# Y-direction hats spread by DMA, weights on VectorE, copies on ScalarE, and 64x64 attention products

## The chip, the cores and the metric

The kernel runs on one core of one Trainium2 chip. The metric is the time of one execution on the device in microseconds (us); lower is better. Engines are named as in the profile: PE is TensorE's matmul, PEld its weight load, DVE is VectorE, ACT is ScalarE, POOL is GpSimd, SP issues the DMAs.

## The reference

The input x is (8, 64, 32, 32): 8 images, 64 channels. Two deformable 3x3 convolutions, then attention and an expert layer on the 1024 pixels of each image as tokens:

```python
off1 = conv2d(x, w_off1, b_off1, stride=1, pad=1)
out = relu(bn_inf(deform_conv(x, off1, w_dc1, 1, 2, 2), g1, beta1, m1, v1))
off2 = conv2d(out, w_off2, b_off2, stride=1, pad=1)
out = relu(bn_inf(deform_conv(out, off2, w_dc2, 1, 2, 2), g2, beta2, m2, v2) + x)
t = to_tokens(out)
t = t + attention(layer_norm(t))      # 8 heads, each token sees the 32 tokens up to its own
t = t + experts(layer_norm(t))        # 32 experts, 8 tokens each per image
```

`deform_conv` reads, for each pixel and each of 9 taps (spaced 2 apart), the image at a place moved by that pixel's own offsets (dy, dx), by bilinear interpolation, and multiplies the 9 samples of 64 channels with a 576x64 matrix.

## The kernel before

**Sampling as a product.** The bilinear weight of a source pixel is a hat in x times a hat in y: with a distance d, min(|d|, 1) - 1 in either direction, so that the signs cancel. The image is cut into tiles of 4 rows by 8 columns (32 pixels, `TR` = 8 tile rows, `TC` = 4 tile columns). A *unit* is one ky of the taps and 4 output rows at most; there are 25 in a convolution, in threes (ky = 1, 0, 2), and three make one row of 4 output rows. A unit has two *strips* in the main (one per tile row that its offsets reach; offsets under 1 pixel are taken for granted, and a flag set by the largest offset leads to a general path `all_*` that does not run here). For each strip:

- `columns_pe` (L186): PE makes x distances into a pair of PSUM banks of a ring of two pairs; ACT takes their absolute value into `hx` (L384), DVE makes the hats (L428).
- `rows_pe` (L204): the same for y distances, with ACT at L390 and DVE at L431. These are made again in every unit, for 128 partitions (32 source pixels by 4 images), though all 8 columns of a source row share them.
- `weigh` (L357): hats in x times hats in y, DVE for one half of the images (g = 0) and POOL for the other (g = 1).
- `sample` (L301): 32 matmuls, source pixels by 64 channels against the weights, into PSUM banks 0 to 3. In the trace an f32 matmul is two records, so a strip is 64.
- `take` (L334): ACT copies banks 0 and 1 to SBUF, DVE banks 2 and 3. The banks are there once, so PE starts the next unit after both.

After the middle unit of a row, from unit 4 on, comes the *final* of the row before (`final_pe`, L234: 36 matmuls, 72 records; the second convolution adds the residual, L241), and ACT applies the normalization (L1418, L1424). In the first convolution PE also turns each finished row into source tiles (L262).

**Order.** Everything is an order written out by hand per engine. `Plan` makes the list of ring items ("x", "y", "f" for final, "t" for turn); PE starts `unit.inside` between the products of a unit and `unit.behind` after them. An item waits for the one two places before it to be emptied (two ring slots). While a unit is sampled, the hats of the second next are made. Ahead of the sampler, `offsets_*` convolve the offsets, split them in three bf16 parts, and move these through DRAM into the layout of `off`.

**Attention.** 32 blocks in a loop of four per turn. A block's PE work is `queries` (L856: 8 products of 64x128 weights), a mask (L869), `scores` (L879: 16 products, 64x128 weights, 64 columns), `values` (L923) for two images, `turn_probs` (L904), `turn_keys` (L892), `project_values` (L938). Blocks overlap: PE turns probabilities one block ahead, scores are further ahead. DVE subtracts the maximum (L1042, L1044) and sums; ACT does the exponential (L991) and copies values (L1003) out of PSUM.

Of the kernel before, what the change touches and what calls it, by code (L numbers as in the profile page):

```python
# [71 lines left out]
class Strip:  # L72


    def __init__(self, tile_row, first, n):
        self.tile_row, self.first, self.n = tile_row, first, n


class Unit:
    def __init__(self, u, strips_before):  # L80
# [4 lines left out]
        for tile_row in range(TR):  # L85
# [3 lines left out]
            if last > first:  # L89
                self.strips.append(Strip(tile_row, first - self.base, last - first))  # L90
# [4 lines left out]
        self.y_items = []  # L95
        for strip in sorted(self.strips, key=lambda strip: -strip.n):
            for item in self.y_items:
                if sum(a.n for a in item) + strip.n <= UNIT_ROWS:
                    item.append(strip)
                    break  # L100
            else:
                self.y_items.append([strip])
        at = 0
        for item in self.y_items:
            for strip in item:
                strip.at = at
                at += strip.n
        self.hat_rows = at
        self.coords = [("x", u, 0), ("x", u, 1)] + [("y", u, k) for k in range(len(self.y_items))]


class Plan:
# [6 lines left out]
    def __init__(self, turns):  # L119
# [6 lines left out]
        for unit in self.units:  # L126
            todo = self.units[unit.u + 2].coords if unit.u + 2 < len(UNITS) else []
            final = [("f", unit.u // 3 - 1)] if unit.u % 3 == 1 and unit.u >= 4 else []
            turn = [("t", unit.u // 3 - 2)] if turns and unit.u % 3 == 1 and unit.u >= 7 else []
            cut = len(todo) if final else (len(todo) + 1) // 2  # L130
            unit.inside, unit.behind = todo[:cut], todo[cut:] + final + turn
            if unit.u == len(UNITS) - 1:
                unit.behind = unit.behind + [("f", TR - 1)]
                if turns:
                    unit.behind = unit.behind + [("t", TR - 2), ("t", TR - 1)]
# [57 lines left out]
def rows_pe(nc, m, cv, bank, u, strips):  # L193

    base, ky = UNITS[u]
    for strip in strips:
        for first, n in offset_parts(base + strip.first, strip.n):
            for g in range(2):
                rows = group_rows(g, 0)
# [1644 lines left out]
```

## Time and profile before

| | us |
|---|---|
| median of 3 runs (725.22 to 732.11) | 725.85 |
| the profiled execution, its span | 730.97, 729.2 |
| loads and first offset convolution | 0 to 37.9 |
| first sampler | 37.9 to 203 |
| second offset convolution | 203 to 232.6 |
| second sampler | 232.6 to 391 |
| layer norm, folded head weights | 391 to 419 |
| attention (its loop from 448) | 419 to 662 |
| experts | 662 to 729 |

The stages are read from the first and last instructions of their lines. PE is busy 80% of the span, DVE 64%, ACT 50%, POOL 40%. The mean granted TensorE clock is 0.865 of the upper level (2.4 GHz); the lower level is half of it, so a mean of 0.75 says that half of the time was spent there.

### The profile page before, as it was taken

How to read it: one execution, taken by the hardware profiler on the slowest of the kernel's cores; microseconds unless marked ns; L12 is line 12 of the kernel's file. 1: busy time of each engine (PE TensorE's matmuls, PEld its weight loads, DVE VectorE, ACT ScalarE, POOL GpSimd, SP SyncE). 2: the span in 40 equal slices, each digit the busy share in tenths (PEclk: the TensorE clock that was granted, in tenths of full speed). 3: DMA queues.
4: the chain of work that ended last, by engine and by line, in shares of the span. 5: the costliest groups of instructions: out<-in, count | busy, mean ns of one | idle time of the engine just before them, and what ended most of it. 6: DMA issues, size and time to landing. Idle time of an engine off the chain costs nothing.

```text
span 729.2 us, 28608 instructions
## 1 busy us (share of the span) xinstructions
PE 584.0 (80%) x12986; PEld 436.3 (60%) x12986; DVE 464.4 (64%) x554; ACT 361.7 (50%) x558; POOL 291.9 (40%) x275
## 2 busy tenths in 40 slices
PE   5668878887875787778776597999999999994556
PEld 1156666665532666556655486888888888873343
DVE  0578877886306889788854525666666766666544
ACT  0265656665214656455552434655656656554522
POOL 4046656665100556665640504344344343330400
PEclk9958979988787589899999556999999999998769
DMA  8320000000004000000001800000000000000002
GB/s 307 75 38 3 4 4 4 4 4 3 4 4 90 12 4 4 3 4 4 4 4 35 234 1 2 3 0 0 0 0 0 0 0 0 0 1 1 1 1 117
DMA packets 6395, 17.85 MB, mean 24 GB/s; under 512 B 1869, under 2 KB 4237, under 8 KB 5573
## 3 DMA queue, kind: packets, MB, share of 16 engines
q1 hardware_dynamic: 6286, 16.24, 8.0%
q8 instruction: 87, 1.43, 0.8%
q14 instruction: 22, 0.18, 0.1%
HBM read 12.37 MB, written 3.87 MB: 22 GB/s over the span
## 4 chain that ended last, share of the span: by engine, by line
PE 63%; DVE 17%; ACT 8%; issue 6%; DMA 3%; POOL 1%; SPq 1%; DVEq 0%; POOLq 0%; ACTq 0%
PE banks L301 13%; PE banks L879 9%; PE banks L234 9%; PE banks L856 5%; PE banks L923 5%; PE banks L904 5%; DVE y L357 5%; PE banks L938 4%; ACT hy L390 3%; DVE y L334 3%; PE banks L650 2%; DMA off<-in_places_dram 2%; DVE hy L431 2%; PE banks L869 2%; ACT hx L384 1%
## 5 line engine op out<-in xcount | busy, mean ns | idle before, releaser
L357 POOL TENSOR_TENSOR y<-hy,hx 128x576 f32<-128x576 f32 (+1 forms) x92 | 166.9, 1832 | 183.4 <-DVE hy L431 180.9
L301 PE MATMUL banks<-y,xt 32*64 32x144 f32 (+1 forms) x5888 | 148.2, 326 | 54.2 <-DVE y L334 42.5
L301 PEld LDWEIGHTS banks<-y,xt 32*64 32x64 f32 x5888 | 126.5, 151 | 71.4 <-issue 54.1
L357 DVE TENSOR_TENSOR y<-hy,hx 128x576 f32<-128x576 f32 (+1 forms) x92 | 113.2, 1268 | 5.1 <-PE banks L301 0.5
L1120 POOL TENSOR_TENSOR y<-y,stats 128x1024 f32<-128x1024 f32 x32 | 60.9, 1902 | 109.1 <-DVE stats L1052 109.0
L384 ACT ACTIVATE hx<-banks 128x576 f32<-128x576 f32 x100 | 65.0, 654 | 67.7 <-PE banks L186 64.6
L1042 DVE TENSOR_REDUCE stats<-banks 128x16 f32<-128x1024 f32 x32 | 39.2, 1225 | 69.5 <-PE banks L879 69.5
L234 PE MATMUL banks<-y,w_dc 64*64 64x256 f32 x1152 | 76.7, 424 | 3.7 <-DVE y L334 2.3
L390 ACT ACTIVATE hy<-banks 128x768 f32<-128x768 f32 (+1 forms) x92 | 70.4, 812 | 14.3 <-PE banks L204 13.9
L334 DVE COPY y<-banks 128x768 f32<-128x768 f32 x50 | 47.6, 952 | 46.6 <-PE banks L301 46.4
L879 PEld LDWEIGHTS banks<-src,y 64*128 64x128 f32 x1024 | 64.5, 201 | 7.9 <-issue 7.9
L879 PE MATMUL banks<-src,y 64*128 64x64 f32 x1024 | 69.1, 289 | 0.0
L1003 ACT COPY hy<-banks 128x512 f32<-128x512 f32 x64 | 38.0, 593 | 62.6 <-PE banks L923 62.6
L234 PEld LDWEIGHTS banks<-y,w_dc 64*64 64x64 f32 x1152 | 47.5, 152 | 30.9 <-issue 12.2
L431 DVE TENSOR_SCALAR hy<-hy 128x1632 f32<-128x1632 f32 (+2 forms) x50 | 45.9, 918 | 11.5 <-ACT hy L390 11.4
L204 PE MATMUL banks<-off,sel 14*64 14x384 bf16 (+1 forms) x384 | 43.5, 378 | 9.5 <-ACT hx L384 7.8
L428 DVE TENSOR_SCALAR hx<-hx 128x1152 f32<-128x1152 f32 x50 | 44.7, 894 | 6.3 <-ACT hx L384 6.3
L991 ACT ACTIVATE y<-y 128x1024 f32<-128x1024 f32 x32 | 33.9, 1059 | 27.1 <-DVE y L1044 27.1
L1050 DVE TENSOR_REDUCE stats<-y 128x16 f32<-128x1024 f32 x32 | 39.0, 1218 | 12.9 <-ACT y L991 12.9
L186 PE MATMUL banks<-off,sel 14*64 14x144 bf16 (+1 forms) x832 | 40.6, 254 | 6.4 <-issue 6.1
L904 PE MATMUL banks<-identity,y 128*128 128x128 f32 x256 | 42.9, 291 | 3.1 <-ACT hy L997 3.1
L923 PE MATMUL banks<-hy 64*64 64x128 f32 x1024 | 42.9, 282 | 1.7 <-ACT hy L1003 1.7
(141 smaller groups left out, 836.1 us busy)
## 6 DMA issues: line engine op xcount, KB each, us to landing
src<-in_x_dram SPq DMA_DIRECT2D x4, 578.0 KB, 5.7
y<-in_w_dram SPq DMA_DIRECT2D x1, 2080.0 KB
xt<-in_xt_dram SPq DMA_DIRECT2D x1, 2048.0 KB, 11.4
off<-in_w_dram SPq DMA_DIRECT2D x2, 1024.0 KB
out_dram<-tokens SPq DMA_DIRECT2D x4, 512.0 KB, 2.6
offsets_dram<-tokens SPq DMA_DIRECT2D x32, 54.0 KB
off<-offsets_dram SPq DMA_DIRECT2D x16, 108.0 KB
w_dc<-in_w_dc_dram SPq DMA_DIRECT2D x2, 288.0 KB, 8.8
```

The costliest lines, as they stand in the source:

```text
L234: last = nc.tensor.matmul(out, cv.w_dc[rows, tap, :], moving, start=(tap == 0), stop=(tap == TAPS - 1 and cv.k == 0), skip_group_check=True)
L301: last = nc.tensor.matmul(ap(out, [[UNIT_ROWS * PITCH - 2, 3], [PITCH, strip.n], [1, WIN_COLS]]), m.xt[32 * j:32 * j + 32, strip.tile_row, ...
L334: return copy(ap(m.sampled[:, unit.ky, unit.slot if unit.ky == 1 else unit.base // UNIT_ROWS % 2, j, 0, :], [[3 * PLACES, 2], [W, 3 * UNIT ...
L357: multiply(dst, hy, hx, ALU.mult).then_inc(cv.s_ready[g], 1)
L384: nc.scalar.activation(ap(m.hx[:, u % 2, 0, side * item[2]:], [[X_HATS, 2], [2 * side, 3], [1, side]]), ap(m.ps[:, bank, :], [[BANK, 2], [ ...
L390: nc.scalar.activation(ap(m.hy[:, u % 2, 0, strips[0].at * HAT_ROW:], [[Y_HATS, 2], [HAT_PITCH, 3 * n_rows], [1, W]]), ap(m.ps[:, bank, :] ...
L428: nc.vector.tensor_scalar(hat, hat, 1.0, 1.0, ALU.min, ALU.subtract).then_inc(cv.hats, 1)
L431: nc.vector.tensor_scalar(hat, hat, 1.0, 1.0, ALU.min, ALU.subtract).then_inc(cv.hats, 1)
L879: last = nc.tensor.matmul(m.ps[:, 2 + hg, first:first + KEYS], at.g[rows, b % 2, image, j, :], keys[rows, b % 4, j * TQ:j * TQ + KEYS], st ...
L904: last = nc.tensor.transpose(m.ps[:, 4, k * P:(k + 1) * P], at.p[:, b % SLOTS_P, hg, image, odd, :], m.identity[:, :])
L923: last = nc.tensor.matmul(m.ps[C * hg:C * hg + C, 5 + late, first:first + P], at.xw[rows, b % 2, odd, C * image:C * image + C], at.pt[rows ...
L1120: nc.gpsimd.tensor_tensor(p, p, scale.unsqueeze(2).to_broadcast([P, 2 * TILES * HG, KEYS]), ALU.mult).then_inc(at.probs_ready, 1)
```

## The change

**Hats in y once per source row.** `rows_pe` and its items are gone. The offsets in f32 go to DRAM as they are (`dump_offsets`), and 96 partitions (4 source rows of a tile, 8 images, 3 kx) read a chunk of 8 output rows; ACT takes |distance| with a bias from a new table `hy_bias` (8 instructions a chunk, 4 chunks), DVE makes the hats (one instruction), SP writes them to DRAM (`write_chunk`) and reads them per unit, each source row's into the partitions of its 8 columns (`read_unit`: two DMAs of 128 x 816 f32, 418 KB each), into three slots.

**Weights and copies.** DVE does all products of `weigh`; POOL none. ACT copies all four banks, but for every third unit, in which DVE copies two.

**Order.** PE samples a unit in one piece; the x items, the final and (one place later than the final) the turn stand behind it.

**Attention.** The products of `queries`, mask and `scores` are halved to 64x64 weights, and PE's waits for queries, scores and the second image's values are gathered before the last transposition of the first image's probabilities.

```diff
-            cut = len(todo) if final else (len(todo) + 1) // 2
-            unit.inside, unit.behind = todo[:cut], todo[cut:] + final + turn
+            row, phase = unit.u // 3 - 1, unit.u % 3
+            final = [("f", row)] if row >= 0 and phase == 1 else []
+            turn = [("t", row)] if turns and row >= 0 and phase == 2 else []
+            unit.inside, unit.behind = [], todo + final + turn
...
         elif item[0] == "f":
-            for taker in range(2):
-                pe.wait_ge(cv.taken[taker], 3 * (item[1] + 1) + 1)
+            pe.wait_ge(cv.taken, 2 * (3 * (item[1] + 1) + 1))
...
+def takers(unit):
+
+    return "av" if unit.u % 3 == 2 else "aa"
+
+
+def weigh(nc, dve, m, cv, unit):
+
+    dve.wait_ge(cv.hy_loaded[unit.u % HAT_SLOTS], 2 * 16 * (unit.u // HAT_SLOTS + 1))
+    dve.wait_ge(cv.hats, unit.u + 1)
+    for strip in unit.strips:
...
+        for g in range(2):
...
+            nc.vector.tensor_tensor(dst, hy, hx, ALU.mult).then_inc(cv.s_ready, 1)
...
-        take(nc.scalar.copy, m, cv, unit, 0).then_inc(cv.taken[0], 1)
+        take(nc.scalar.copy, m, cv, unit, 0).then_inc(cv.taken, 1)
+        if takers(unit) == "aa":
+            take(nc.scalar.copy, m, cv, unit, 2).then_inc(cv.taken, 1)
         for _ in unit.behind:
             item_act(n)
             n += 1
+        chunk, step = divmod(unit.u, UNITS_PER_CHUNK)
+        if chunk + 1 < CHUNKS_Y and step < 2:
+            chunk_distances(nc, act, m, cv, chunk + 1, step)
...
+    for row in range(TILE_ROWS):
+        col = 2 * row + lower
+        nc.scalar.activation(
+            ap(m.hat[0:COMPACT, row * ROW_HATS + lower * HAT_ROW:], [[TILE_ROWS * ROW_HATS, 2], [HAT_PITCH, 3], [1, W]]),
+            ap(m.hyin[0:COMPACT, row * W:], [[TILE_ROWS * W, 2], [CHUNK_ROWS * W, 3], [1, W]]),
+            ACT.Abs, bias=m.hy_bias[0:COMPACT, col:col + 1]).then_inc(cv.near, 1)
...
+        if bank == 1:
...
+            for lower in range(2):
+                chunk_distances(nc, act, m, cv, 0, lower)
...
+    def read_unit(u):
...
+            sp.wait_ge(cv.s_ready, 2 * cv.plan.units[u - HAT_SLOTS + 1].before)
...
+            source = bass.AP(at.tensor, at.offset, [[plane, 16], [0, TILE_COLS], [1, n * ROW_HATS]])
+            sp.dma_start(m.hy[:, u % HAT_SLOTS, g, first * ROW_HATS:(first + n) * ROW_HATS], source
+                         ).then_inc(cv.hy_loaded[u % HAT_SLOTS], 16)
...
-                    last = nc.tensor.matmul(m.ps[:, 2 + hg, first:first + KEYS], at.g[rows, b % 2, image, j, :],
-                                            keys[rows, b % 4, j * TQ:j * TQ + KEYS], start=False, stop=True,
-                                            skip_group_check=True)
+                    for side in range(2):
+                        half = slice(C * side, C * side + C)
+                        last = nc.tensor.matmul(m.ps[half, 2 + hg, first:first + KEYS], at.g[rows, b % 2, image, j, half],
+                                                keys[rows, b % 4, j * TQ:j * TQ + KEYS], start=False, stop=True,
+                                                skip_group_check=True)
...
+    def before_products(i, b):
+
+        if exists(i, b + QUERIES_AHEAD):
+            before_queries(i, b + QUERIES_AHEAD)
+        if exists(i, b + SCORES_AHEAD):
+            before_scores(i, b + SCORES_AHEAD)
+        before_values(i, b, 1)
```

Line numbers move: L301 becomes L271, L186 L183, L234 L208, L334 L298, L384 L353, L428 L407, L357 L328; in attention L856 becomes L914, L869 L933, L879 L943, L923 L989, L904 L970. New are L391 (ACT, chunk distances) and L400 (DVE, chunk hats).

DVE in the second sampler, one unit, before: `hx` and `hy` hats, two weights (the other two are POOL's), the copy.

```order
L428 TENSOR_SCALAR hx<-hx 128x1152 [waits c1_emptied]
L431 TENSOR_SCALAR hy<-hy 128x1632 [waits c1_emptied]
L357 TENSOR_TENSOR y<-hy,hx 128x576 [waits c1_hats,c1_sampled]
L357 TENSOR_TENSOR y<-hy,hx 128x576 [waits c1_sampled]
L334 COPY y<-banks 128x768 [waits c1_sampled]
```

And now, two units; the semaphores `c1_hy_loaded0` to `2` are the DMA's into the three slots:

```order
L407 TENSOR_SCALAR hx<-hx 128x1152 [waits c1_emptied]
L328 TENSOR_TENSOR y<-hy,hx 128x576 [waits c1_sampled,c1_hats,c1_hy_loaded2]
L328 TENSOR_TENSOR y<-hy,hx 128x576
L328 TENSOR_TENSOR y<-hy,hx 128x576 [waits c1_sampled]
L328 TENSOR_TENSOR y<-hy,hx 128x576
L407 TENSOR_SCALAR hx<-hx 128x1152 [waits c1_emptied]
L328 TENSOR_TENSOR y<-hy,hx 128x576 [waits c1_sampled,c1_hats,c1_hy_loaded0]
L328 TENSOR_TENSOR y<-hy,hx 128x576
L328 TENSOR_TENSOR y<-hy,hx 128x576 [waits c1_sampled]
L328 TENSOR_TENSOR y<-hy,hx 128x576
L298 COPY y<-banks 128x768 [waits c1_sampled]
```

The `hy` hats are gone from DVE, the products are four instead of two, and the copy stands in one unit of three.

PE around a final of the second sampler before (L234); `banks<-y,xt` are samplings, `banks<-off,sel` distances:

```order
L301 MATMUL banks<-y,xt 64x3x4x12 [waits c1_s_ready1,c1_s_ready0]
L301 MATMUL banks<-y,xt 64x3x4x12 x15
L204 MATMUL banks<-off,sel 64x3x2x32 [waits c1_emptied]
L204 MATMUL banks<-off,sel 64x3x2x32 x7
L301 MATMUL banks<-y,xt 64x3x4x12 x16
L204 MATMUL banks<-off,sel 64x3x2x32 [waits c1_emptied]
L204 MATMUL banks<-off,sel 64x3x2x32 x7
L234 MATMUL banks<-y,w_dc 64x2x128 [waits c1_taken1,c1_taken0,c1_emptied]
```

And the same place now:

```order
L271 MATMUL banks<-y,xt 64x3x4x12 [waits c1_s_ready]
L271 MATMUL banks<-y,xt 64x3x4x12 x31
L183 MATMUL banks<-off,sel 64x3x24 [waits c1_moved1,c1_emptied]
L183 MATMUL banks<-off,sel 64x3x24 x15
L183 MATMUL banks<-off,sel 64x3x24 [waits c1_emptied]
L183 MATMUL banks<-off,sel 64x3x24 x15
L208 MATMUL banks<-y,w_dc 64x2x128 [waits c1_taken,c1_emptied]
```

The distances no longer stand between samplings, and the ring slot that the final waits for (`c1_emptied`) is now the first x item's of the same unit, which ACT empties after its copies.

PE in the attention loop before, from the queries to the scores:

```order
L856 MATMUL banks<-src,s 128x128 [waits at_z_ready,at_xw_ready,at_pt_ready]
L923 MATMUL banks<-hy 64x128 x8
L900 REGISTER_ALU [waits at_probs_ready]
L904 MATMUL banks<-identity,y 128x128 [waits at_pt_ready]
L904 MATMUL banks<-identity,y 128x128 x3
L863 REGISTER_ALU
L869 MATMUL banks<-mask,spread_q 128x512 [waits at_shifted,at_swapped_ready,at_g_ready]
L869 MATMUL banks<-mask,spread_q 128x512
L879 MATMUL banks<-src,y 128x64 x15
L910 REGISTER_ALU
L879 MATMUL banks<-src,y 128x64 [waits at_z_ready,at_pt_ready]
L923 MATMUL banks<-hy 64x128 x8
```

And now:

```order
L970 MATMUL banks<-identity,y 128x128 [waits at_pt_ready]
L970 MATMUL banks<-identity,y 128x128 x2
L903 REGISTER_ALU
L905 ISA [waits at_windows_ready]
L922 ISA [waits at_g_ready]
L976 ISA [waits at_shifted,at_swapped_ready,at_g_ready]
L970 MATMUL banks<-identity,y 128x128 [waits at_z_ready,at_pt_ready]
L914 MATMUL banks<-src,s 64x128 x16
L933 MATMUL banks<-mask,spread_q 64x512 x4
L943 MATMUL banks<-src,y 64x64 x32
```

The wait for `z_ready`, ACT's copy of the first image's values, stood at the last score product; it now stands before queries, mask and all scores.

## Rows read from the trace of the kernel before

**Rows 1.** Windows: us, PE, PEld, DVE, ACT, POOL busy, PEclk, DMA share, GB/s

```profile
8.00:12.00 4.00, 1.11 (x16) 0.44 (x24) 0.00 (x0) 0.00 (x0) 0.71 (x1) 1.00 1.06 441
66.89:184.29 117.40, 95.27 (x3206) 71.94 (x3204) 91.87 (x89) 68.00 (x100) 71.58 (x60) 0.86 0.02 4
264.03:377.54 113.51, 88.63 (x3232) 67.25 (x3232) 91.79 (x89) 64.69 (x95) 65.92 (x36) 0.92 0.02 4
419.40:448.00 28.60, 23.91 (x180) 19.96 (x180) 12.10 (x14) 9.12 (x13) 5.09 (x9) 0.50 0.01 1
448.00:640.00 192.00, 192.00 (x2966) 156.99 (x2966) 124.07 (x163) 115.67 (x194) 78.20 (x110) 0.99 0.00 0
```

**Rows 2.** Timeline, one row of the second sampler: start, us, instruction [idle <-releaser]

```profile
288.27 0.96 DVE L334 COPY y<-banks 128x768 f32<-128x768 f32 x1 [0.36 <-PE banks L301]
...
289.01 1.54 ACT L390 ACTIVATE hy<-banks 128x768 f32<-128x768 f32 x2
...
290.58 1.01 DVE L431 TENSOR_SCALAR hy<-hy 128x1632 f32<-128x1632 f32 x1 [0.69 <-ACT hy L390]
...
291.70 2.56 DVE L357 TENSOR_TENSOR y<-hy,hx 128x576 f32<-128x576 f32 x2
...
295.22 0.78 PE L301 MATMUL banks<-y,xt 32*64 32x144 f32 x32 [2.70 <-DVE y L334]
```

**Rows 3.** Groups by shape, ACT: busy us, mean ns of one | idle before

```profile
L384 ACT ACTIVATE hx<-banks 128x576 f32<-128x576 f32 x100 | 65.0, 654 | 67.7 <-PE banks L186 64.6 <-PE banks L204 1.2
...
L334 ACT COPY y<-banks 128x768 f32<-128x768 f32 x50 | 39.7, 794 | 8.3 <-PE banks L301 8.3
...
L1003 ACT COPY hy<-banks 128x512 f32<-128x512 f32 x64 | 38.0, 593 | 62.6 <-PE banks L923 62.6
```

**Rows 4.** Timeline, weight loads of finals (L234), the loads behind one

```profile
66.89 0.30 PEld L234 LDWEIGHTS banks<-y,w_dc 64*64 64x64 f32 x8 [0.52 <-ACT hy L390]
...
184.29 0.30 PEld L234 LDWEIGHTS banks<-y,w_dc 64*64 64x64 f32 x8 [0.38 <-issue]
...
185.21 0.25 PEld L234 LDWEIGHTS banks<-y,w_dc 64*64 64x64 f32 x4 [0.18 <-issue]
...
264.03 3.66 PEld L234 LDWEIGHTS banks<-y,w_dc 64*64 64x64 f32 x72 [0.62 <-ACT hy L390]
...
268.51 0.48 PEld L301 LDWEIGHTS banks<-y,xt 32*64 32x64 f32 x32 [0.39 <-issue]
```

**Rows 5.** Timeline, weight loads of sampling (L301), 32 in one piece, twice

```profile
50.59 0.84 PEld L301 LDWEIGHTS banks<-y,xt 32*64 32x64 f32 x32 [2.33 <-issue]
...
289.30 0.51 PEld L301 LDWEIGHTS banks<-y,xt 32*64 32x64 f32 x32 [0.70 <-ACT y L334]
```

**Rows 6.** Timeline, DVE, a weights product while POOL runs none

```profile
374.92 0.76 DVE L357 TENSOR_TENSOR y<-hy,hx 128x576 f32<-128x576 f32 x1
```

**Rows 7.** Timeline, one turn of the attention loop

```profile
502.25 0.43 PEld L923 LDWEIGHTS banks<-hy 64*64 64x64 f32 x16
...
507.28 1.86 PEld L879 LDWEIGHTS banks<-src,y 64*128 64x128 f32 x32 [0.23 <-issue]
...
509.21 0.42 PEld L923 LDWEIGHTS banks<-hy 64*64 64x64 f32 x16
...
509.33 1.22 DVE L1042 TENSOR_REDUCE stats<-banks 128x16 f32<-128x1024 f32 x1 [1.84 <-PE banks L879]
...
510.59 1.22 DVE L1044 TENSOR_TENSOR y<-banks,stats 128x1024 f32<-128x1024 f32 x1
...
511.63 0.97 PEld L856 LDWEIGHTS banks<-src,s 64*128 64x128 f32 x16 [0.17 <-issue]
...
511.84 1.06 ACT L991 ACTIVATE y<-y 128x1024 f32<-128x1024 f32 x1 [0.76 <-DVE y L1044]
```

**Rows 8.** Timeline, weight loads of the folded head weights, 64 columns each

```profile
396.51 0.54 PEld L1742 LDWEIGHTS banks<-y 64*64 64x64 f32 x16 [1.29 <-DMA y<-in_w_attn_dram]
```

**Rows 9.** Timeline, first scores ahead of the attention loop

```profile
425.31 3.49 PEld L879 LDWEIGHTS banks<-src,y 64*128 64x128 f32 x32 [0.44 <-issue]
```

More of the change, by code:

```diff
@@ L93, in __init__ @@
             strip.count = strips_before + k
[L95 to L109, printed above, removed]
+        rows = [strip.first for strip in self.strips] + [strip.first + strip.n for strip in self.strips]
+        self.hat_first, self.hat_end = min(rows), max(rows)
+        self.coords = [("x", u, 0), ("x", u, 1)]
 class Plan:
@@ L190, in columns_pe @@
     last.then_inc(cv.filled, 1)
[L193 to L199, printed above, removed]
-                at = offset_at(3 * ky, first)
-                to = 3 * W * (strip.at % UNIT_ROWS + first - base - strip.first)
-                for side in range(2):
-                    half = slice(C * side, C * side + C)
-                    last = nc.tensor.matmul(
-                        ap(m.ps[half, bank + g, to:], [[W, 3], [3 * W, n], [1, W]]),
-                        m.sel[rows, strip.tile_row, half], ap(m.off_flat[rows, at:], [[HALF_PIX, 3], [W, n], [1, W]]),
-                        start=True, stop=True, skip_group_check=True)
-    last.then_inc(cv.filled, 1)
 def sampled_rows(m, rows, row, pair, tap):
@@ L428, in hats @@
         nc.vector.tensor_scalar(hat, hat, 1.0, 1.0, ALU.min, ALU.subtract).then_inc(cv.hats, 1)
[L429 to L435 removed]
     units = cv.plan.units
     hats(units[0])
[L439 removed]
+    weigh(nc, dve, m, cv, units[0])
     hats(units[1])
@@ L702 @@
-MOVES = 4 * 16
+            read_parts(half, g, 0, cv.moved_y)
+    for u in range(HAT_SLOTS, len(UNITS)):
+        chunk = u // UNITS_PER_CHUNK
+        if u % UNITS_PER_CHUNK == 0 and chunk < CHUNKS_Y:
+            write_chunk(chunk)
+            if chunk + 1 < CHUNKS_Y:
+                read_chunk(chunk + 1)
+        read_unit(u)
+    for slot in range(HAT_SLOTS):
+        sp.wait_ge(cv.hy_loaded[slot], 2 * 16 * len(range(slot, len(UNITS), HAT_SLOTS)))
+    sp.wait_ge(cv.moved_y, 2 * MOVES)
@@ L705 @@
+MOVES = 2 * 16
 CONV1_LOADS = 16 * 10
@@ L866, in scores @@
             pe.wait_ge(at.shifted, i * BODY + b)
+    def scores(b):
         for hg in range(HG):
-            rows = slice(TQ * hg, TQ * hg + TQ)
-            nc.tensor.matmul(m.ps[:, 2 + hg, :], m.spread_q[rows, :], m.mask[rows, :], start=True, stop=False,
-                             skip_group_check=True)
+            rows = slice(C * hg, C * hg + C)
+            for side in range(2):
+                half = slice(C * side, C * side + C)
+                nc.tensor.matmul(m.ps[half, 2 + hg, :], m.spread_q[rows, half], m.mask[rows, :], start=True, stop=False,
+                                 skip_group_check=True)
         for image in range(2):
```

318 lines of the change are left out of this document (191 added, 127 removed).

## The prediction

> **What bounds the kernel now.** I read the windows first, for the granted clock by stage, then the finals in the timeline, since one final stands in each row of a sampler and their distance is the pace, then what PE waited for between two of them, and last one turn of the attention loop.
>
> The pace: in the first sampler six rows pass from 66.89 to 184.29, 19.57 us each; in the second 264.03 to 377.54, 18.92 each [rows 1, 4]. Neither PE nor DVE is full: PE 95.3 of 117.4 and 88.6 of 113.5, DVE 91.9 and 91.8 [rows 1]. The timeline says why. A unit runs through a chain: ACT's two absolute values of y (1.54), DVE's hats in y (1.01, after a wait for ACT), two weights on DVE (2.56) beside POOL's, the copy on DVE (0.96), and only then PE's next sampling, which stood 2.70 us idle for that copy [rows 2]. A DVE product takes 0.76 when POOL runs none and 1.28 beside it [rows 2, 6]. So the bound is DVE's serial work, mostly hats in y and slowed products.
>
> In the attention loop a block takes 6.96 (502.25 to 509.21), at clock 0.99 with PE busy 192.0 of 192.0 [rows 1, 7]: PE bounds it, scores being its longest piece with 1.86. Ahead of the loop the clock is 0.50 and scores take 3.49 [rows 1, 9].
>
> **The samplers, part by part.** Gone per unit: 1.54 of ACT, 1.01 of DVE, the y distances of PE, and all of POOL. Added: two products on DVE. DVE per row of three units: 12 products of 0.76, three hats of at most 1.01, one copy of 0.96, 13.1 in all [rows 2, 6], under the row that follows, so DVE stops being the bound. What is left is PE and the copies in turn, because banks 0 to 3 are there once. At the upper clock:
>
> - Sampling a unit: two strips of 64 loads at 0.51/32 = 16 ns, 2.04 [rows 5], and 0.27 until the last product ends (0.78 against 0.51 for 32 [rows 2, 5]): 2.3.
> - First unit of a row: 2.3, two ACT copies in turn at 0.79 [rows 3], and 0.1 for handing over (estimate; the waits of 0.05 to 0.17 in these views): 4.0.
> - Middle unit: 4.0, then ACT's absolute value of the first x item, 0.65 [rows 3], because the final now waits for the ring slot of that item, behind the copies on ACT; 0.1; then final, residual and turnaround, 4.48 (264.03 to 268.51 [rows 4]): 9.2. The x items of PE lie beside the copies and cost nothing there; without that cover they would be some 0.3 a unit.
> - Last unit: 2.3 + 0.96 + 0.1 = 3.4, the DVE copy [rows 2] running beside ACT's.
>
> Sum 16.6 for the second sampler. The first lacks the residual (0.4), but its turn waits for an absolute value and runs itself (1.05): 17.25.
>
> At the lower clock a sampling load takes 0.84/32 = 26 ns [rows 5], 1.3 a unit more, and a final's group of four 0.43 (0.25 and a gap of 0.18 [rows 4]), 7.7 for 72 against 3.66: about 8 more a row, 24.6 and 25.25. Which clock will be granted no row of the changed kernel's kind shows. The bounds are 1.00 and 0.50; I take the share of time of before, 28% at the lower level in the first sampler (0.86) and 16% in the second (0.92) [rows 1], as PE's share of work in a row stays near. That makes 21% and 11% of the work: 18.93 and 17.5. Six rows each: -3.8 and -8.5.
>
> ACT copies both pairs in turn, 1.58, where ACT and DVE side by side took 0.96 [rows 2, 3]: two units in three pay 0.6. The Trainium skill, TensorEngine Tiling (Array Packing), PSUM Bottleneck, says to use both ScalarE and VectorE to empty PSUM, which speaks against this edit. By that advice the samplers would come out some 15 us lower (2 x 0.6 x 12 rows) if DVE had the time; it is inside my sum as a price paid.
>
> **Their starts and ends.** ACT's eight chunk distances now stand before the last two banks of offsets. One has 192 columns; from 0.65 for 576 and 0.79 for 768 [rows 3] I estimate 0.37, so 3.0 with no cover, twice. Against it the five units ahead of the first final win like others (0.5 to 0.8 each): +1 a sampler, bounds -3 to +5. The later chunks put four such instructions, 1.5, behind the copies in five units of each sampler; in the middle units they hide under the final, in the others about 0.7 comes through: +1 each. At the end, two copies in turn before the last final: +1 each. Together +6.
>
> The DMA: 835 KB a unit in at most 5.5 us (16.6/3) asks for 152 GB/s; the start of the kernel shows 441 [rows 1], so 1.9 us, two units ahead of use. I cost it at nothing; if that cover is gone, see the rivals. SP has no other work there but writing and reading chunks. The bias table is a small load among many at the start: nothing.
>
> **Attention.** The halved products: a 64x64 load with 128 columns takes 0.42/16 = 27 ns [rows 7], so queries 32 x 27 = 0.85 instead of 0.97. For scores with 64 columns the nearest row is 27 ns too, but there both tiles of a pair use the same input rows [rows 8]; in the scores input rows alternate as well, so four tiles can run where two did. Sampling loads come at 16 ns [rows 5], so loads as such are no floor at 27. I take half, 13.5: scores 0.86 instead of 1.86; ends 13.5 and 27.
>
> PE then needs 5.8 a block and another chain ends last: scores end, DVE's two steps 2.48, exponential 1.06, ACT's copy of values 0.59 [rows 3, 7], the last transposition and PE's turnaround 0.3 (0.17 of it [rows 7]), queries 0.85, mask 0.35 (estimate, its turnaround 0.23 [rows 7] and four products), scores 0.86, drain and hand-overs 0.3: 6.8. The wait for the copied values, moved ahead of queries, mask and scores, is what puts those on the chain; queued behind it on PE are also the second image's values and the projection. Some 28 blocks by 0.16: -4.5. Ahead of the loop, at the lower clock, three scores of 3.49 [rows 9] become 64 x 27 ns = 1.73, and queries gain 0.1 each: -5.7. Together -10.2, ends -16 and +20.
>
> **Sum.** -12.3 + 6 - 10.2 = -16.5. The profiled execution took 730.97 (median of runs 725.85, so its own excess of 5 is left out of the forecast): 714.5 for one like it, 709 for the median.
>
> **Rivals.**
>
> *The clock falls in the samplers; slower.* Place: PE between samplings, where it now stands still 1.7 us in two of three units with the x items done, instead of taking distances in between; with the final behind an absolute value too. Every row then costs up to 24.6 and 25.25. The change of the whole is -32 + 48 x (s1 + s2), s being the shares of work at the lower clock, 0.21 and 0.11 in my sum. It decides from s = 0.33 each, a mean clock of about 0.79; from 0.41, a clock of about 0.75, it is slower by over 1%; wholly at the lower level 790. For it: the clock was 0.50 ahead of the attention loop, where PE stood in gaps, though busy 23.9 of 28.6 [rows 1]. Against: PE's busy share before was little higher than it will be and 0.86 to 0.92 was granted. Time if it happens 733 to 790.
>
> *The half products give nothing.* If 27 ns holds for scores too, they take 1.73, the chain grows to 7.65, and the loop loses 0.7 x 28 = 20: 739. For it: 64x128 loads took 58 ns for 64 columns and 61 for 128 [rows 7], as if the load, not the columns, set the pace; against it the 16 ns of sampling. The Trainium skill, TensorEngine Tiling (Array Packing), Instruction Overhead, puts some 60 cycles on every matmul of trn2, an estimate of 25 ns at 2.4 GHz, which would give nearly this rival's time; the 16 ns of a sampling load [rows 5] do not agree with that as a floor where several tiles run.
>
> *The clock stays up in the samplers.* 17.25 and 16.6: another 15 us off, 693.
>
> *The spread DMA is late.* It decides below 152 GB/s: at 100, 8.4 us a unit, 25 units twice, over 800. Against: 441 GB/s with the queues full [rows 1]; but there partitions got longer pieces.
>
> *The hats are not hidden because the order isn't as I read it*, the weights of the second strip coming after PE wants them: up to 1 us a row, 721, no change by the measure of 1%, which is about what can be told here.
>
> **Chances and range.** Forecast (694 to 719) 0.52, clock up 0.09, no change from weights or a clock between 0.15, clock down 0.13, half products without gain 0.09, DMA 0.02. Faster by over 1% (below 718.6) 0.61, within 0.15, slower 0.24. The range from 689, between forecast and clock up, to 742, which holds the second rival and the upper part of the first: 0.2 outside.
>
> **What would show it.** Finals 18.9 and 17.5 apart with PE waiting for ACT's copy, not DVE's; weights at 0.7 to 0.76 on DVE; no wait of DVE for the DMA; clock 0.86 and 0.92 in the same stretches; scores of 0.86 and a block of 6.8 with PE idle before the last transposition. Wrong it would be by a clock below 0.8, a score near 1.7, or weights that wait for hats.

## The result, and the profile after

774.36 us, median of 4 runs, beside 728.62: ratio 1.062, interval 1.053 to 1.070. Three of the runs took 771.89 to 775.92; the fourth, 1601.25 at a clock of 1.00, is not explained; the median counts it (772.8 without it), the ratio does not. The kernel became slower by 6%; the forecast was 709, the range ended at 742.

Cut at the same marks, the span of 771.0 stands to 729.2 like this ("to the first final" is the *ramp* below: from a sampler's first sampling to its first final):

| stretch | before | after | change |
|---|---|---|---|
| to the first sampling | 41.4 | 50.1 | +8.7 |
| to the first final | 25.5 | 32.2 | +6.7 |
| six rows | 117.4 | 126.8 | +9.4 |
| to the first sampling of the second sampler | 53.3 | 60.6 | +7.4 |
| to its first final | 26.5 | 33.5 | +7.0 |
| six rows | 113.5 | 128.0 | +14.5 |
| rest: attention and experts | 351.7 | 339.8 | -11.9 |

Starts and ramps together lose 29.8, the rows 23.9, and the rest gains 11.9.

The windows of the changed kernel (columns as in [rows 1]): the ramp of the first sampler, the six rows of each, the attention loop.

```profile
44.00:82.31 38.31, 17.27 (x624) 14.89 (x624) 19.21 (x28) 16.91 (x31) 0.00 (x0) 0.63 0.86 216
82.31:209.11 126.80, 94.33 (x3064) 75.52 (x3064) 69.59 (x97) 56.09 (x95) 6.28 (x24) 0.84 0.50 129
303.22:431.20 127.98, 93.47 (x3089) 74.07 (x3089) 69.34 (x96) 51.99 (x89) 0.00 (x0) 0.85 0.50 127
470.00:690.00 220.00, 185.01 (x4898) 150.59 (x4900) 140.28 (x184) 135.64 (x216) 90.32 (x128) 0.96 0.01 5
```

In the rows POOL is nearly empty now and DVE has dropped from 91.9 to 69.6, as meant; PE is no fuller than before. The clock went from 0.86 and 0.92 to 0.84 and 0.85. The new column to look at is DMA: half of the 16 engines' time in the rows and 0.86 in the ramp, for 129 and 216 GB/s.

**The start**, in the timeline: offsets are dumped, read back, made into hats, written, and read again by unit.

```profile
25.25 0.38 SPq L683 DMA_DIRECT2D offsets_dram<-y  x1
...
27.95 2.99 SPq L702 DMA_DIRECT2D s<-offsets_dram  x4
...
33.25 2.87 ACT L391 ACTIVATE s<-s,hy_bias 96x192 f32<-96x192 f32 x8 [7.46 <-DMA s<-offsets_dram]
...
36.03 0.67 ACT L646 ACTIVATE y<-banks,b_off 128x512 f32<-128x512 f32 x1
...
38.30 3.10 SPq L708 DMA_DIRECT2D hats_dram<-s  x4
...
45.31 3.84 SPq L722 DMA_DIRECT2D hy<-hats_dram  x6
...
49.14 0.83 DVE L328 TENSOR_TENSOR y<-hy,hx 128x288 f32<-128x288 f32 x2 [1.83 <-DMA hy<-hats_dram]
...
50.12 1.36 PE L271 MATMUL banks<-y,xt 32*64 32x72 f32 x64 [3.09 <-DVE y L328]
```

From the dump at 25.25 to the first weights at 49.14 the hats travel for 24 us, through four DMAs one behind the other, and the first sampling waits for them. ACT stood waiting for the offsets with two banks of its own work behind it (L646 at 36.03).

**The ramp.** ACT's rows after the second unit, and PE's sampling that waited:

```profile
52.95 1.21 ACT L353 ACTIVATE hx<-banks 128x576 f32<-128x576 f32 x2
...
62.26 1.49 ACT L391 ACTIVATE s<-s,hy_bias 96x192 f32<-96x192 f32 x4 [8.09 <-DMA s<-offsets_dram]
...
63.66 1.47 ACT L298 COPY y<-banks 128x768 f32<-128x768 f32 x2
...
65.18 3.40 PEld L271 LDWEIGHTS banks<-y,xt 32*64 32x64 f32 x113 [5.55 <-ACT y L298]
```

The distances of the second chunk (L391) stand ahead of the copies in ACT's order. They waited for their offsets until 62.26; the copies of a unit that PE had sampled by then came at 63.66, and PE stood 5.55. DVE waited for hats too, seven times, and all seven lie in the starts and ramps:

```profile
DVE y L328 <- DMA hy<-hats_dram: 15.3, 7, 3.5
```

(A line of waits: us in total, times, longest.)

**A row with chunk work**, from final to final, 23.1 us:

```profile
324.63 0.56 PEld L208 LDWEIGHTS banks<-y,w_dc 64*64 64x64 f32 x12 [2.07 <-ACT hx L353]
...
325.36 0.26 PEld L208 LDWEIGHTS banks<-y,w_dc 64*64 64x64 f32 x4 [0.16 <-issue]
...
330.94 0.69 ACT L1521 ACTIVATE tokens<-banks,bn_shift 128x512 f32<-128x512 f32 x1 [5.82 <-PE banks L215]
...
331.53 1.48 ACT L391 ACTIVATE s<-s,hy_bias 96x192 f32<-96x192 f32 x4
...
333.04 1.01 DVE L400 TENSOR_SCALAR s<-s 96x1632 f32<-96x1632 f32 x1 [7.12 <-ACT s L391]
...
333.97 2.75 DVE L328 TENSOR_TENSOR y<-hy,hx 128x576 f32<-128x576 f32 x4
...
336.64 0.95 DVE L298 COPY y<-banks 128x768 f32<-128x768 f32 x1
...
337.64 2.36 PEld L271 LDWEIGHTS banks<-y,xt 32*64 32x64 f32 x99 [4.40 <-DVE y L298]
...
347.76 0.21 PEld L208 LDWEIGHTS banks<-y,w_dc 64*64 64x64 f32 x8 [1.99 <-ACT hx L353]
```

ACT takes the chunk's distances behind the final's own emptying (330.94), DVE waited for them in the chunk's hats until 333.04, its weights and its copy stood behind that, and PE waited 4.40 for the copy. The final itself is slow after its first 12 loads, 0.42 for each group of four. Rows 2 and 4 of each sampler look like that.

**Attention.** One turn of the loop: scores' end, the last transposition, queries, scores, and scores' end again.

```profile
561.03 1.23 DVE L1124 TENSOR_REDUCE stats<-banks 128x16 f32<-128x1024 f32 x1 [1.63 <-PE banks L943]
...
565.23 0.30 PE L970 MATMUL banks<-identity,y 128*128 128x128 f32 x1 [0.92 <-ACT hy L1085]
...
565.46 0.86 PEld L914 LDWEIGHTS banks<-src,s 64*64 64x64 f32 x32
...
566.60 1.11 PE L943 MATMUL banks<-src,y 64*64 64x64 f32 x64
...
567.48 0.43 PEld L989 LDWEIGHTS banks<-hy 64*64 64x64 f32 x16
...
567.78 1.23 DVE L1124 TENSOR_REDUCE stats<-banks 128x16 f32<-128x1024 f32 x1 [1.63 <-PE banks L943]
```

A block takes 6.75, from DVE's reduction to the next, where it took 6.96 [rows 7]; PE waits 0.92 for ACT's copy: the chain that I drew.

### The profile page after: what moved, and what is told of

Read it like the earlier page. It is cut to its first block, busy times and chain, and to the rows that moved or that the text cites. A ratio compares the mean times of both kernels' runs of the same rounds, so it can differ in the third digit from the quotient of the medians.

```text
span 771.0 us, 31010 instructions
## 1 busy us (share of the span) xinstructions
PE 535.8 (70%) x14202; PEld 404.7 (52%) x14202; DVE 403.3 (52%) x570; ACT 342.2 (44%) x564; POOL 122.9 (16%) x183
## 4 chain that ended last, share of the span: by engine, by line
PE 25%; DVE 14%; ACT 6%; issue 4%; POOL 1%; ACTq 0%; DVEq 0%
PE banks L914 5%; PE banks L943 4%; DVE stats L1124 4%; DVE y L1126 4%; PE banks L208 3%; PE banks L271 3%; ACT hy L1085 2%; PE banks L970 2%; PE banks L989 2%; PE banks L1014 1%; DVE norm_stats L847 1%; PE banks L933 1%; ACT y L1073 1%; ACT y L298 1%; PE banks L807 1%
## 5 line engine op out<-in xcount | busy, mean ns | idle before, releaser
L271 PE MATMUL banks<-y,xt 32*64 32x144 f32 (+1 forms) x5888 | 134.8, 331 | 72.3 <-ACT y L298 30.2
L271 PEld LDWEIGHTS banks<-y,xt 32*64 32x64 f32 x5888 | 116.6, 157 | 89.5 <-ACT y L298 33.6
L328 DVE TENSOR_TENSOR y<-hy,hx 128x576 f32<-128x576 f32 (+1 forms) x184 | 125.1, 740 | 18.9 <-DMA hy<-hats_dram 15.3
L298 ACT COPY y<-banks 128x768 f32<-128x768 f32 x84 | 63.7, 800 | 106.7 <-PE banks L271 106.7
L208 PE MATMUL banks<-y,w_dc 64*64 64x256 f32 x1152 | 88.4, 470 | 30.1 <-ACT hx L353 26.7
L208 PEld LDWEIGHTS banks<-y,w_dc 64*64 64x64 f32 x1152 | 55.9, 166 | 57.9 <-ACT hx L353 29.1
L407 DVE TENSOR_SCALAR hx<-hx 128x1152 f32<-128x1152 f32 x50 | 37.9, 758 | 71.4 <-ACT hx L353 71.4
L970 PE MATMUL banks<-identity,y 128*128 128x128 f32 x256 | 49.0, 295 | 30.6 <-ACT hy L1085 27.0
L353 ACT ACTIVATE hx<-banks 128x576 f32<-128x576 f32 x100 | 60.3, 664 | 13.0 <-PE banks L183 13.0
L970 PEld LDWEIGHTS banks<-identity,y 128*128 128x128 f32 x256 | 28.2, 142 | 48.7 <-issue 43.7
L1085 ACT COPY hy<-banks 128x512 f32<-128x512 f32 x64 | 36.9, 577 | 20.1 <-PE banks L989 20.1
L1079 ACT COPY hy<-banks 128x512 f32<-128x512 f32 x64 | 37.5, 586 | 17.5 <-PE banks L970 17.3
L1067 ACT COPY y<-banks 128x512 f32<-128x512 f32 x64 | 34.4, 589 | 19.8 <-PE banks L914 19.8
L989 PE MATMUL banks<-hy 64*64 64x128 f32 x1024 | 41.8, 279 | 0.9 <-ACT hy L1085 0.9
L1126 DVE TENSOR_TENSOR y<-banks,stats 128x1024 f32<-128x1024 f32 x32 | 39.2, 1224 | 1.1
L298 DVE COPY y<-banks 128x768 f32<-128x768 f32 x16 | 15.3, 955 | 46.7 <-PE banks L271 46.7
L635 PE MATMUL banks<-src,w_off 64*18 64x512 f32 x576 | 34.8, 640 | 6.7 <-DMA src<-in_x_dram 6.7
## 6 DMA issues: line engine op xcount, KB each, us to landing
xt<-in_xt_dram SPq DMA_DIRECT2D x1, 2048.0 KB, 11.4
```

What stands on the lines that cost most here:

```text
L208: last = nc.tensor.matmul(out, cv.w_dc[rows, tap, :], moving, start=(tap == 0), stop=(tap == TAPS - 1 and cv.k == 0), skip_group_check=True)
L271: last = nc.tensor.matmul(ap(out, [[UNIT_ROWS * PITCH - 2, 3], [PITCH, strip.n], [1, WIN_COLS]]), m.xt[32 * j:32 * j + 32, strip.tile_row, ...
L298: return copy(ap(m.sampled[:, unit.ky, unit.slot if unit.ky == 1 else unit.base // UNIT_ROWS % 2, j, 0, :], [[3 * PLACES, 2], [W, 3 * UNIT ...
L328: nc.vector.tensor_tensor(dst, hy, hx, ALU.mult).then_inc(cv.s_ready, 1)
L353: nc.scalar.activation(ap(m.hx[:, u % 2, 0, side * item[2]:], [[X_HATS, 2], [2 * side, 3], [1, side]]), ap(m.ps[:, bank, :], [[BANK, 2], [ ...
L970: last = nc.tensor.transpose(m.ps[:, 4, k * P:(k + 1) * P], at.p[:, b % SLOTS_P, hg, image, odd, :], m.identity[:, :])
```

## The experiments

Times are medians; the kernel before stood at 729 to 731 in the same sessions. "Rows" are the six rows between the first and the seventh final of a sampler.

**The attention alone, on the kernel before** (the diff's attention part, nothing else).

> The kernel before with the new attention alone. In the changed kernel's trace the stretch from the seventh final of the second sampler to the end is 339.8 us against 351.7 before. If the 64x64 products and the gathered waits bring that by themselves, this kernel is 12 us faster than before: 714 to 718 beside 728. The rival, that the gain came with another state of PE's clock or queue after the samplers: 723 to 728, no change.

716.8, ratio to before 0.982 (0.976 to 0.988). The gain is the attention's own, 13 us. So the rest of the change costs 57.

**Chunk work at other places.**

```diff
+        for item in unit.behind:
+            if early and item[0] == "f":
+                chunk_distances(nc, act, m, cv, chunk + 1, step)
...
+        if unit.u == 3:
+            chunk_hats(nc, dve, m, cv, 1)
```

> The changed kernel (774 us) with its chunk work at other places of the same engines' orders: ACT takes the distances of the second half of a chunk before it empties the final, the chunk after the first is made two units later, and SP reads the next chunk's offsets after the unit's hats. Nothing is left out. My theory, that ACT waiting for offsets from DRAM (5.5 us of PE waiting once a sampler) and DVE waiting in chunk_hats behind the final (4.4 instead of 1.0, twice a sampler) carry a good part of the loss: 12 us a sampler less, 750, within 745 to 756. The rival, that the spread DMA or the clock carries the loss wherever the chunk work stands: 769 to 777.

770.4, near the rival. Rows 2 and 4 of the first sampler fell from 22.8 and 23.4 to 20.5 and 21.1 as expected, but the first rows took 25.2 and 26.1 instead of 20.8 and 21.4, and the ramp stayed (32.6, 34.7). In these first rows PE stops once for 3.97 and once for 4.98 without a wait (what such stops are is shown with the run without later chunks), so their length does not tell what the second chunk costs at its new place. Where the work stands matters, and no place that I gave it is free.

**Copies split in every unit.**

```diff
-    return "av" if unit.u % 3 == 2 else "aa"
+    return "av"
```

> The changed kernel with the copies of every unit split, ACT two banks and DVE two banks. If the two ACT copies in turn are on the chain and the idle time that they leave PE lowers the clock: 1.2 us a row by 15 rows at least, 757, and to 742 where the clock rises too. The rival, that DVE has no time and its copy stands behind weights: 772 or above.

766.7, between the two; not decided here, see the run without DMA below.

**No spread after the first three slots.** Later units use what lies there.

```diff
...
-        read_unit(u)
...
```

> The changed kernel with hats in y read from DRAM for three slots only, at the start of each sampler; all later units use what lies there, so their hats are those of other rows. The chunk work and its writes stay. If the 835 KB per unit are the main cost (DMA engines 90% busy where PE stalls, late hats, late instruction loads): below 748. If they cost only the stalls of PE that the timeline shows in two rows of each sampler (about 1.9 each): 764 to 770. If nothing: 774.

752.2, between two of the ranges: more than the stalls that I counted. Rows without chunk work fall to 18.4 and 18.1, rows with it stay at 22.7 and 23.

**PE kept busy.** The first x item made three times over.

```diff
-            columns_pe(nc, m, cv, bank, item[1], item[2])
+            columns_pe(nc, m, cv, bank, item[1], item[2], 3 if item[2] == 0 else 1)
```

> The changed kernel, in which PE makes the first x item of each unit three times over (16 or 32 products more a unit, into the same place, so the result is the same), while it would otherwise stand waiting for ACT's copies. It adds work to PE and takes none away. If the idle time before the finals and samplings is what lowers the clock there (finals whose groups of four take 0.43, 3.5 for 128 sampling loads instead of 2.0), the time falls: 745 to 762, with a mean clock above 0.86. The rival, that the clock does not hang on these gaps: 776 to 790, the added products showing.

801.1, above both ranges, with a clock of 0.81 in the rows:

```profile
82.67:220.28 137.61, 101.25 (x3368) 80.87 (x3369) 69.35 (x97) 56.54 (x95) 6.29 (x24) 0.81 0.46 119
```

This does not decide on my theory of the clock, because the run did not fill PE's gaps: PE stood idle for 36.4 of the first sampler's six rows, where the changed kernel has 32.5. Of that, 16.4 are stops without a wait (3.1 in the changed kernel).

**No later chunks.** All units read rows of the first chunk.

```diff
-CHUNKS_Y, UNITS_PER_CHUNK = H // CHUNK_ROWS, 6
+CHUNKS_Y, UNITS_PER_CHUNK = 1, 6
...
```

> The changed kernel with the hats of the first chunk alone: the distances, hats, writes and reads of chunks two to four are left out, and later units read rows of the first chunk, as many bytes as before. If the chunk work on ACT and DVE is what it seems in the timeline (ACT waiting for offsets in the ramp, 5.5, and two rows a sampler longer by 4.3): 28 us less than 774, 742 to 752. The rival, that moving it only shifted the wait because the spread DMA is late behind it: 764 to 772.

751.0, as expected: 23 us for the chunk work. What is left is seen best in this run. PE's weight loads in one sampling, and windows around them:

```profile
144.23 1.71 PEld L271 LDWEIGHTS banks<-y,xt 32*64 32x64 f32 x107 [0.39 <-issue]
...
147.98 0.32 PEld L271 LDWEIGHTS banks<-y,xt 32*64 32x64 f32 x18 [2.05 <-issue]
```

```profile
144.20:145.90 1.70, 1.70 (x106) 1.67 (x107) 0.00 (x0) 0.79 (x1) 0.71 (x3) 1.00 0.83 152
145.90:148.00 2.10, 0.32 (x22) 0.05 (x6) 0.00 (x0) 0.00 (x0) 0.34 (x2) 1.00 0.96 277
148.00:150.00 2.00, 0.97 (x38) 0.78 (x37) 0.96 (x1) 1.26 (x3) 0.00 (x0) 0.91 0.35 90
150.00:158.00 8.00, 6.53 (x269) 6.01 (x276) 4.28 (x6) 3.81 (x7) 0.00 (x0) 0.81 0.30 73
```

After 107 of 128 loads, in the middle of a strip, where no semaphore is waited for, PE stops for 2.05; ACT and DVE have nothing to do, and only the DMA engines are busy, 0.96 at 277 GB/s. Then the clock is down to 0.81.

What PE waits for can be read from the DMA queues. One of them carries instructions (packets, MB, share of the engines). First the changed kernel, then the run further below in which PE makes 832 products more:

```profile
q8 instruction: 85, 1.39, 0.8%
...
q8 instruction: 92, 1.51, 0.9%
```

Its packets are of 16 KB. In six rows PE passes some 255 loads and products for each packet, so a packet is worth about 256 of 64 bytes (an estimate), and the 832 products with their loads fit the seven packets more. In all sixteen traces, over the rows of both samplers, there are 137 stops of over 0.45 before a load that waits for no semaphore. Every one of them ends 1.2 to 1.7 us after the end of such a packet, though packets come only every 4.7 us. So in these stops PE waits for its own instructions. Here the packet ended at 146.40 and the stop at 147.98. In the run with an eighth of the bytes, whose PE program is the same, the same packet began 185 loads and products earlier in the program: the hats' bytes delay it.

But the stops are not new. The kernel before has 6.2 and 5.9 us of them in its rows, with the DMA engines at 0.02, and the changed kernel 3.1 and 5.5. One of them, in the kernel before:

```profile
97.81 0.13 PEld L301 LDWEIGHTS banks<-y,xt 32*64 32x64 f32 x1 [1.76 <-issue]
```

**Neither.**

> The changed kernel with neither later chunks nor hats read after the first three slots (both edits of the runs before together; later hats are those of other rows). What is left is PE, ACT's copies, DVE's weights and the first chunk. If the two costs add: 722 to 732, rows of 17.3 to 18. If they overlap (the same wait counted twice): 738 to 748.

714.0, 8 below the lower end. 22 and 23 alone, 60 together: taking out one gains more once the other is gone. Why is not shown. Its windows:

```profile
76.04:179.37 103.33, 76.89 (x3064) 62.50 (x3064) 68.13 (x95) 50.80 (x79) 6.31 (x24) 0.97 0.02 4
263.68:373.77 110.09, 85.71 (x3088) 68.52 (x3089) 68.14 (x95) 46.68 (x73) 0.00 (x0) 0.89 0.02 4
```

The rows of the first sampler are 16.67 in four of six, at 0.97; in the second they are 16.1 to 20.0, at 0.89.

**The first chunk behind all offsets**, `if bank == 1` becoming `if bank == 3` on ACT and DVE.

> The changed kernel with the first chunk's distances and hats behind the last two banks of offsets on ACT and DVE, so that these banks no longer wait for offsets to come back from DRAM. If the way of the first hats through DRAM (dump, read, write, spread) sets the first sampling: no change, 771 to 776. If ACT's queue sets it, the first sampling comes some 6 us earlier in both samplings: 760 to 764.

773.5: no change. The first sampling comes 2 us earlier (48.1), not 6. The way through DRAM sets most of the start.

**An eighth of the bytes**, on the kernel without later chunks.

```diff
+        width = n * ROW_HATS if u < HAT_SLOTS else n * ROW_HATS // 8
...
-            source = bass.AP(at.tensor, at.offset, [[plane, 16], [0, TILE_COLS], [1, n * ROW_HATS]])
+            source = bass.AP(at.tensor, at.offset, [[plane, 16], [0, TILE_COLS], [1, width]])
...
```

> The kernel without later chunks, in which the DMAs of hats stand in the same number and at the same places, but from the fourth unit on carry an eighth of the bytes; the rest of each slot keeps what the first three units read, so later hats are those of other rows. If it is the bytes, which keep the DMA engines busy: as without the spread, 713 to 722 (714.0 there). If it is the number of DMAs, their issue on SP and the waits for them: 742 to 752 (751.0 with all bytes).

718.8 (713 to 726) against 751.0 (748 to 758): it is the bytes. PE's weight loads of a whole row, and the windows of its rows:

```profile
111.49 3.66 PEld L208 LDWEIGHTS banks<-y,w_dc 64*64 64x64 f32 x72 [1.99 <-ACT hx L353]
...
115.53 2.00 PEld L271 LDWEIGHTS banks<-y,xt 32*64 32x64 f32 x128 [0.39 <-issue]
...
119.85 2.00 PEld L271 LDWEIGHTS banks<-y,xt 32*64 32x64 f32 x128 [0.17 <-issue]
...
123.72 2.00 PEld L271 LDWEIGHTS banks<-y,xt 32*64 32x64 f32 x128 [1.51 <-ACT y L298]
...
128.16 3.66 PEld L208 LDWEIGHTS banks<-y,w_dc 64*64 64x64 f32 x72 [2.07 <-ACT hx L353]
```

```profile
78.16:178.40 100.24, 73.82 (x3064) 61.08 (x3064) 68.09 (x95) 50.78 (x79) 6.30 (x24) 1.00 0.09 21
267.39:369.48 102.09, 77.70 (x3088) 62.75 (x3088) 68.09 (x95) 46.67 (x73) 0.00 (x0) 0.97 0.09 21
```

Final to final 16.67: 3.66 for a final, 2.00 for a sampling, nothing slow. The same windows with all bytes:

```profile
80.83:198.13 117.30, 86.58 (x3064) 69.08 (x3065) 68.14 (x95) 50.79 (x79) 6.29 (x24) 0.91 0.48 121
291.13:405.34 114.21, 85.36 (x3088) 66.22 (x3089) 67.85 (x94) 46.68 (x73) 0.00 (x0) 0.93 0.48 124
```

The rows win 29 us. PE is idle 9 us less, which the stops make up (12 between weight loads), and busy 20 us less for the same work, at a higher clock. The wait of 2.0 before each final is still there and the clock is 1.00 and 0.97.

**Copies split, without the later DMAs** (the kernel of *Neither*).

> The kernel with neither later chunks nor spread after the first three slots (714.0), with the copies of every unit split between ACT and DVE. The chain of sampling, copies and final is what is left there (rows of 16.66), so two copies of 0.6 a row less should show: 696 to 704. The rival, that DVE's copy then stands behind its weights: 711 to 718.

710.8, ratio to before 0.976 (0.967 to 0.984) beside 714.0 (0.976, 0.969 to 0.983): the rival, no gain that can be told from noise. Rows stay at 16.56 and 17.00, and PE waits for the copy on DVE:

```profile
PE banks L271 <- DVE y L298: 47.9, 27, 3.0
```

**The parts that need no DMA, on the kernel before**: attention, all weights on DVE, ACT copying all banks in two units of three.

```diff
-            weigh(nc.gpsimd.tensor_tensor, pool, m, cv, unit, strip, 1)
...
+            for g in range(2):
+                weigh(nc.vector.tensor_tensor, dve, m, cv, unit, strip, g)
...
+        if unit.u % 3 != 2:
+            take(nc.scalar.copy, m, cv, unit, 2).then_inc(cv.taken[1], 1)
...
```

> The kernel before with those parts of the change that need no DMA: the new attention, all weights on DVE, ACT copying all four banks in two units of three. The y hats are made per unit as before. If DVE's products slowed beside POOL bound the samplers, and the chain on PE and ACT is shorter: 696 to 710. If ACT, which still takes the absolute values of y (1.54 a unit), now stands in the chain with its copies: 715 to 728.

700.7. Taken again, with an interval:

> The same kernel as the one with the parts of the change that need no DMA (700.65 there, 693 to 705), for an interval: 3 to 5 per cent below the kernel before, 694 to 706. A ratio above 0.98 would mean that its gain over the new attention alone (0.982) is not real.

698.2, ratio 0.956 (0.952 to 0.960): the fastest version of all. Its rows take 103.5 and 106.3 for six, no more than those of *Neither* (103.3 and 110.1) and 3 to 4 more than with an eighth of the bytes. What makes it faster than both lies mostly ahead of the rows: its first finals come at 66.6 and, after the seventh, 78.3 later; with an eighth of the bytes at 78.2 and 89.0. Windows of the first of its two runs:

```profile
66.65:170.13 103.48, 87.17 (x3208) 66.85 (x3205) 84.97 (x115) 75.28 (x112) 8.79 (x24) 0.95 0.02 4
248.46:354.72 106.26, 89.42 (x3234) 66.86 (x3232) 85.19 (x117) 72.70 (x107) 0.00 (x0) 0.92 0.02 4
```

**The same without ACT's additional copies.**

> The kernel before with the new attention and all weights on DVE, copies split as before; POOL makes none. DVE has 12 products of 0.76, six hats of 1.0 and three copies of 0.96 a row, 18.0, against rows of 19.2 before: 704 to 714 if DVE's sum is the bound. If the order on DVE (copies behind weights) makes PE wait longer: 717 to 730.

723.1, ratio 0.989 (0.984 to 0.994): the rival, and no better than the attention alone (0.982). PE waits for DVE's copy:

```profile
PE banks L301 <- DVE y L334: 43.5, 30, 3.4
```

So moving the weights to DVE gained only once most of its copies had left it: 25 us between these two kernels. ACT's additional copies with POOL's weights left as they were have not been run, so how much of the gain needs both is open.

**PE busy, without the later DMAs** (on the kernel of *Neither*).

> The kernel with neither later chunks nor spread after the first three slots (714.0; later hats are those of other rows), and PE making the first x item of each unit three times over as in the run that took 801. There PE stood without a cause in the profile for 16.4 and 11.8 us in the two samplers' six rows, against 3.1 and 7.3 in the changed kernel, while it had 832 instructions more. If these stands are PE's instructions arriving late behind the hats' bytes, they are gone here and the added products hide beside the copies: 708 to 722. If the added products themselves cost it, as 27 us did there: 732 to 745.

736.4: the rival by the time. Its windows:

```profile
78.37:189.87 111.50, 85.59 (x3368) 69.03 (x3368) 68.12 (x95) 51.17 (x79) 6.29 (x24) 0.95 0.02 4
277.66:385.13 107.47, 84.90 (x3393) 68.28 (x3393) 68.13 (x95) 47.07 (x73) 0.00 (x0) 0.97 0.02 4
```

In the first sampler a row takes 18.6 instead of 16.67, and of the 1.9 more 1.5 are stops, mostly of 1.2 to 1.8, each ending behind an instruction packet (8.9 in its rows, 7.8 in the second's). So the stops need no hats' bytes: 832 more products bring them too. The rows of the second sampler are 2.6 shorter than without the added products, at 0.97 instead of 0.89; the rest of the profiled run's 13.7 more lies mostly in the ramps. (Counted over the six rows alone, the expectation's 11.8 and 7.3 are 8.9 and 5.5.)

## Why the prediction was wrong, step by step

**The sum, term by term.** Rows: +23.9 instead of -12.3. Starts and ramps: +29.8, where starts, chunks and ends had +6 together. Attention and the rest: -11.9 instead of -10.2.

**The chain on PE and ACT: right.** I walked a row at 17.25 and 16.6 at the upper clock. With an eighth of the bytes and no later chunks it takes 16.67 in the first sampler and 16.2 to 18.4 in the second. That this kernel takes 719 and *Neither* 714, beside my 709, is luck in part: the clock in the rows came out higher than I took it (1.00 and 0.97 with an eighth of the bytes), and the start takes some 20 us more than before in both samplers together. DVE is busy 68.1 in six rows there, 11.4 each, under my 13.1. My walk has no term for the stops for instructions, 1.0 us a row in the kernel before.

**"The DMA ... I cost it at nothing": this failed first.** I took 441 GB/s from loads of long pieces and 1.9 us a unit. The spread ran at 216 GB/s with the engines 0.86 busy in the ramp, and it cost 22 us with the chunk work in place (774.4 to 752.2) and 32 without (751.0 to 718.8). My rival of the late DMA named the right resource, but its mechanism, hats that come late, holds for the starts and ramps alone, where all seven of DVE's waits lie. In the steady rows no hats are late; there the bytes hold up PE's instructions. Stops of over 0.45 add up to 4.8 and 7.9 us in the rows without later chunks, and 0 to 0.5 where the bytes are gone too. In the changed kernel they are 3.1 and 5.5, less than the 6.2 and 5.9 of the kernel before, so the stops explain what the bytes cost beside a kernel without them, but not why the rows became longer than before. Beside the stops, PE takes longer for the same work in these rows, at a lower clock; that the stops cause the lower clock is not shown (the run with PE busy and no bytes has more stops, at 0.95 and 0.97).

**"+1 each" for the chunks: mis-sized, 23 instead of 2** (38 where the spread is gone, 752.2 to 714.0). I costed four instructions of 0.37 and found them a place beside the final. Their time was right (1.48 for four). What I left out is waiting in order: ACT's wait for a DMA with copies behind it, DVE's wait for ACT with weights and a copy behind it.

**"3.0 with no cover" for the start: +8.7 and +7.4.** I costed ACT's instructions and not the way of the data through four DMAs. The run with the first chunk moved shows that the way decides most of it: without that work ahead of ACT's last banks the first sampling came only 2 us earlier.

**The ramps, forecast to win, lost 6.7 and 7.0.** To the first final, start and ramp together, the changed kernel needs 82.3 and 94.1 beside 66.9 and 79.7 before. Without later chunks it is 80.8 and 93.0, with an eighth of the bytes as well 78.2 and 89.0. So ACT's wait of 8.1 in the trace is worth little, with all chunk work 1.5 and 1.1: without it DVE waits 5.0 for hats there. The bytes are worth 2.7 and 4.0. Some 20 of the 30 us are left. They are gone where the y hats are made per unit as before (66.6 and 78.3), so I put them down to the first chunk's way through DRAM; no run has that way shortened.

**The clock: its cause stays open.** I made its fall a rival with PE's waits for the copies as the cause. The waits came as drawn, 2.07 before each final, and with them and an eighth of the bytes the clock was 1.00 and 0.97: they alone do not lower it. In the rows it was 0.81 to 0.93 in every run that had the hats' bytes; but it was 0.86 and 0.92 in the kernel before, 0.87 and 0.88 with chunk work and no spread, and 0.89 in the second sampler of the run without either, so the bytes are not the one cause. By the prediction's own price of 48 us for the shares of work, 0.84 and 0.85 mean shares of 0.24 and 0.22 instead of 0.21 and 0.11, some 7 us (an estimate) of the 65 that the forecast missed. The price per row at the lower clock was right in kind: finals at 0.42 a group.

**Copies in turn, "a price paid" of 15 us: it was none.** Splitting them gave nothing that shows without the later DMAs, and on the kernel before, with the weights on DVE, it cost 25; in the changed kernel as it is, 766.7 stood beside 774.4, with ratios whose intervals just overlap. The Trainium skill, TensorEngine Tiling (Array Packing), PSUM Bottleneck, says to use both engines to empty PSUM. These runs do not agree for this kernel: the second engine's copy stands in order behind its own products, so it comes later than a second copy on the first.

**Attention: right.** -10.2 forecast, -11.9 by the trace, -13 alone; the block 6.8 forecast and 6.75. Scores came out at 14 ns a load (64 in 0.88, from 566.60 to the next loads at 567.48), so half products did gain. The Trainium skill, TensorEngine Tiling (Array Packing), Instruction Overhead, has some 60 cycles a matmul, an estimate of 25 ns at 2.4 GHz; taken as a floor on the distance of two products, that does not agree with these 14 ns.

## What to carry to other kernels

A short instruction in an in-order queue costs the wait ahead of it, and that wait is paid by what stands behind it; for each one that waits for a DMA or another engine, name the next that others need. Price a repeated DMA at the rate that pieces of its own shape reach, and ask what else the DMA engines serve while it runs: here PE's own instructions, which the profile lists as a queue. Before a slow stretch is put down to a change, look for the same stretch in the kernel before. Which engine should empty PSUM depends on what stands before the copy in its order: one free engine twice was better than two of which one is busy.

## What the runs showed of the hardware

PE stopped for 0.5 to 5.0 us in the middle of runs of matmuls that wait for no semaphore, and each of 137 such stops ended 1.2 to 1.7 us after a packet of 16 KB on the instruction queue. One such stop fell where the DMA engines were 0.96 busy at 277 GB/s; with an eighth of the bytes 0 to 0.5 us of them were left in six rows, and with 832 more PE matmuls and hardly any bytes they came back, mostly 1.2 to 1.8 each. The kernel before has them with the DMA engines at 0.02. A sampling of 128 loads and 128 products, one packet's worth, took 2.00 at the upper clock; from the start of the packet to the end of a stop it was 2.2 to 3.2. Waits of 2.0 before every final left the clock at 1.00.
